# Attention in steps of two heads: row-tiled score matmuls and three rotating bank pairs, in a rewritten program

## The reference

```python
qkv = (x @ Wqkv.T + bqkv)                       # q, k, v: 16 heads of 16
attn = softmax(q @ k.T / 4)                     # 512 x 512 for each head and batch
coh = sigmoid(tanh([x, cond] @ Wc1.T + bc1) @ Wc2.T + bc2)
mod = attn * coh / ((attn * coh).sum(-1) + 1e-8)
fa = softmax(layernorm(relu(cond @ We1.T + be1) @ We2.T + be2) @ pe.T)   # a row per batch
out = (0.79 * mod + 0.21 * fa) @ v @ Wout.T + bout
x = x + out
x = x + rotate(x)      # a fixed 4 x 4 map of quarter features; the FFT pair with a real gate is a scale
```

## Time and profile before

| | us |
|---|---|
| median of 3 runs | 379.95 |
| lowest, highest | 377.29, 383.14 |
| the profiled execution, span from first to last instruction | 375.9 |
| mean granted TensorE clock in it | 0.904 of full |
| TensorE busy | 321.0 |
| VectorE busy | 223.9 |
| ScalarE busy | 176.9 |
| GpSimd busy | 156.8 |

### The profile page before, as it was taken

How to read it: one execution, slowest core, us unless ns; L and a number is a source line. 1 busy time by engine, 2 the same in 40 slices (tenths; PEclk the granted TensorE clock), 3 DMA queues, 4 the chain that set the end, 5 groups by cost and what they waited for, 6 DMA issues and landing times.

```text
span 375.9 us, 5338 instructions
## 1 busy us (share of the span) xinstructions
PE 321.0 (85%) x1537; PEld 189.0 (50%) x1537; DVE 223.9 (60%) x385; ACT 176.9 (47%) x323; POOL 156.8 (42%) x129
## 2 busy tenths in 40 slices
PE   0848849999799889999799689999799779999975
PEld 0634426555456456655456356655456346544423
DVE  3765943786568616687577407686577517775102
ACT  2101103765356625556456415565356525667750
POOL 9979950099991000299400000199500030296000
PEclk9986975999989958999899958999899969999996
DMA  8698498214953992216924991125943990200001
GB/s 245 247 125 99 146 127 123 83 58 99 125 59 112 126 163 51 75 66 127 124 30 145 149 118 36 62 78 112 118 51 122 124 146 1 84 1 2 1 1 57
DMA packets 16518, 35.87 MB, mean 95 GB/s; under 512 B 2724, under 2 KB 8228, under 8 KB 14456
## 3 DMA queue, kind: packets, MB, share of 16 engines
q1 hardware_dynamic: 14968, 34.47, 50.4%
q10 hardware_dynamic: 1536, 1.23, 1.2%
HBM read 25.07 MB, written 10.50 MB: 95 GB/s over the span
## 4 chain that ended last, share of the span: by engine, by line
PE 63%; DMA 24%; DVE 4%; ACT 3%; issue 3%; SPq 1%; ACTq 0%; DVEq 0%
PE smax_ps L996 14%; PE st_ps L1018 14%; PE o_ps L1030 13%; DMA stack<-max_rows 10%; DMA stack<-qk_scratch 10%; PE job_ps L894 9%; PE job_ps L929 3%; PE job_ps L970 3%; ACT probs L594 2%; DMA qk_scratch<-qk_lo 2%; PE job_ps L951 2%; DVE qk_lo L672 2%; PE smax_ps L982 2%; DMA w_raw<-wqkvT 1%; DVE maxima L746 1%
## 5 line engine op out<-in xcount | busy, mean ns | idle before, releaser
L746 DVE TENSOR_REDUCE maxima<-smax_ps 128x1 f32<-128x512 f32 x256 | 168.3, 686 | 113.6 <-PE smax_ps L996 113.0
L594 ACT ACTIVATE probs<-st_ps 128x512 f32<-128x512 f32 x247 | 142.6, 597 | 137.0 <-PE st_ps L1018 135.6
L996 PE MATMUL smax_ps<-stack 127*128 127x512 f32 x256 | 118.0, 464 | 13.8 <-DMA stack<-qk_scratch 11.9
L1018 PE MATMUL st_ps<-stack 128*128 128x512 f32 x247 | 107.7, 439 | 19.8 <-DMA stack<-max_rows 18.2
L996 PEld LDWEIGHTS smax_ps<-stack 127*128 127x128 f32 x256 | 52.0, 204 | 51.5 <-DVE maxima L746 24.4
L1030 PE MATMUL o_ps<-probs,vals 128*32 128x512 f32 x512 | 71.7, 634 | 1.0 <-ACT probs L594 0.9
L1018 PEld LDWEIGHTS st_ps<-stack 128*128 128x128 f32 x247 | 50.5, 205 | 39.6 <-DMA stack<-max_rows 19.8
L419 POOL TENSOR_TENSOR vals<-v_new,vals 128x256 f32<-128x256 f32 x16 | 10.0, 641 | 94.5 <-PE o_ps L1030 94.5
L401 POOL TENSOR_TENSOR x_lo<-x_raw,x_hi 128x1024 fp32r<-128x1024 f32 x3 | 7.2, 2388 | 65.7 <-ACT x_hi L550 65.7
L894 PE MATMUL job_ps<-x_hi,w_hi 128*128 128x512 f32 x48 | 22.0, 459 | 10.0 <-DVE w_lo L797 9.5
L519 POOL TENSOR_TENSOR prod<-amap,x_tok 128x1024 f32<-128x1024 f32 x12 | 28.6, 2383 | 0.9
(11 more groups left out here) (105 smaller groups left out, 305.5 us busy)
## 6 DMA issues: line engine op xcount, KB each, us to landing
stack<-qk_scratch SPq DMA_DIRECT2D x64, 256.0 KB, 9.7
qk_scratch<-qk_hi SPq DMA_DIRECT2D x16, 256.0 KB, 2.0
qk_scratch<-qk_lo SPq DMA_DIRECT2D x16, 256.0 KB, 2.0
x_tok<-x SPq DMA_DIRECT2D x4, 512.0 KB, 12.0
out<-y SPq DMA_DIRECT2D x8, 256.0 KB, 2.2
x_raw<-xT SPq DMA_DIRECT2D x3, 512.0 KB, 12.1
pe_tab<-fa_rows SPq DMA_DIRECT2D x4, 256.0 KB, 3.8
row<-rows SPq DMA_DIRECT2D x1, 936.0 KB, 7.6
```

The costliest lines, as they stand in the source:

```text
L594: nc.scalar.activation(probs[:, t % RING, :], st_bank(b, t)[:, :], ACT.Exp, scale=SCALE).then_inc(exp_done, 1)
L746: nc.vector.tensor_reduce(maxima[:, g % 2, n:n + 1], smax_ps[smax_bank(u)][:, :], AX_X, ALU.max).then_inc(smax_reduced, 1)
L996: nc.tensor.matmul(smax_ps[smax_bank(u)][:, :], stack[0:MAX_ROW, 0, h, i * P:(i + 1) * P], stack[0:MAX_ROW, 1, h, :], start=True, stop=Tru ...
L1018: nc.tensor.matmul(st_bank(b, t)[:, :], stack[:, 1, h, j * P:(j + 1) * P], stack[:, 0, h, :], start=True, stop=True).then_inc(st_filled, 1)
```

## The change

Nearly every function is rewritten; the computation stays.

- A step is now a pair of heads and one block of 128 rows: 32 steps a batch, 128 in all, unrolled for the four batches. There are 12 steps (`LEAD`) between S and T of the same index.
- `stack` holds two heads in one block: 48 rows (three combinations, lo-lo left out) from partition 0 and 48 from partition 64; T takes a 49th row, the maximum. A pair is two matmuls, one at each partition offset, into the two banks of a pair. Three pairs (`pair_ps`) rotate over the sequence T, S, T, S, ...; in a step T comes first. `slot_free` makes each wait for the reader of the pair used three events earlier.
- One reduce and one exponential cover both banks (1024 elements). The reduce negates.
- One bank `job_ps` for all jobs. Jobs are whole (no thirds) and placed by `JOB_STEPS` and `FIRST_STEPS`, behind the score matmuls and `weigh_values` of their step. `claim` waits for the readout of the job just before. For the jobs in `LATE` VectorE's readout comes one step later, behind that step's reduce.
- `stack` has three slots of half a batch (8 heads); a half is read with six DMAs of 256 KB and one semaphore.
- The first two pairs of heads of batch 0 are projected directly into `stack` (`direct`, plain fp32 from `w_dir`, low parts by two VectorE operations on 16 rows), so S can start without the trip through DRAM.
- The weights are split by GpSimd, not VectorE; the copies of `values` and others go to ScalarE. The logits `z` are computed transposed in four column tiles and transposed back (`zt`). The last batch's output is done whole at the end.

The core of the diff:

```diff
+PER_BATCH = G * IT * 2
+STEPS = B * PER_BATCH
+LEAD = 12
+TERMS = 3
+ROWS = TERMS * HD
+HALF_SLOTS = 3
+JOB_STEPS = {"q0": -20, "k0": -18, "q1": -6, "k1": -4, "v0": -2, "v1": 4, "coh0": 6, "coh1": 10, "z": 11, "zt": 13,
+             "max0": 9, "max1": 17, "max2": 25, "max3": 33, "field": 27,
+             "tok0": 24, "tok1": 32, "tok2": 40, "tok3": 48, "back0": 34, "back1": 50, "out0": 52, "out1": 54}
+FIRST_STEPS = {"q0": 0, "k0": 1, "dq1": 2, "dk1": 3, "q1": 4, "k1": 5, "cond": 6, "norms": 7, "fpre": 8, "v0": 9,
+               "v1": 11, "fpair": 14, "flog": 15, "coh0": 16, "coh1": 18, "z": 19, "zt": 21}
+BEFORE = ["dq0", "dk0"]
+LATE = ("q0", "q1", "k0", "k1", "out0", "out1")
+def weigh_at(n):
+    k, odd = divmod(n - LEAD - 3, 2)
+    return k if not odd and 0 <= k < STEPS // 2 else None
+def events():
+    order = []
+    for n in range(STEPS + LEAD):
+        if n >= LEAD:
+            order.append(("T", n - LEAD))
+        if n < STEPS:
+            order.append(("S", n))
+    return order
+EVENTS = events()
+SLOT = {event: n % 3 for n, event in enumerate(EVENTS)}
+AHEAD = {event: EVENTS[n - 3] for n, event in enumerate(EVENTS) if n >= 3}
...
+            def claim(job):
+                if PLACE[job]:
+                    wait(pe, *read_out(ORDER[PLACE[job] - 1]))
...
+            def slot_free(event):
+                if event in AHEAD:
+                    kind, n = AHEAD[event]
+                    pe.wait_ge(s_reduced if kind == "S" else exp_done, n + 1)
+
+            def scores_for_max(u):
+                gg, pair, i = u // 8, u % 8 // IT, u % IT
+                slot, turn = slot_of(gg // 2)
+                p = 4 * slot + 2 * (gg % 2) + pair
+                if gg == 0:
+                    if i == 0:
+                        pe.wait_ge(dir_lo_done, 4 * (pair + 1))
+                elif u % 16 == 0 or u == 8:
+                    pe.wait_ge(stack_loaded[slot], 96 * (turn + 1))
+                slot_free(("S", u))
+                for a in range(2):
+                    ins = nc.tensor.matmul(pair_ps[SLOT["S", u]][:, a, :],
+                                           stack[64 * a:64 * a + ROWS, 0, p, i * P:(i + 1) * P],
+                                           stack[64 * a:64 * a + ROWS, 1, p, :], start=True, stop=True)
+                ins.then_inc(s_filled, 1)
+
+            def scores(t):
+                gg, j, pair = t // 8, t % 8 // 2, t % 2
+                slot, _ = slot_of(gg // 2)
+                p = 4 * slot + 2 * (gg % 2) + pair
+                if t % 8 == 0:
+                    pe.wait_ge(max_loaded, 16 * (gg + 1))
+                slot_free(("T", t))
+                for a in range(2):
+                    ins = nc.tensor.matmul(pair_ps[SLOT["T", t]][:, a, :],
+                                           stack[64 * a:64 * a + ROWS + 1, 1, p, j * P:(j + 1) * P],
+                                           stack[64 * a:64 * a + ROWS + 1, 0, p, :], start=True, stop=True)
+                ins.then_inc(t_filled, 1)
...
+            for n in range(LAST_STEP + 1):
+                if LEAD <= n < STEPS + LEAD:
+                    scores(n - LEAD)
+                if n < STEPS:
+                    scores_for_max(n)
+                k = weigh_at(n)
+                if k is not None:
+                    weigh_values(k)
+                for job in JOBS.get(n, []):
+                    run_job(job)
```

The new readers and the order of SyncE's work:

```diff
+                nc.vector.tensor_reduce(maxima[:, gg % 2, :, pair, i], pair_ps[SLOT["S", u]][:, :, :], AX_X,
+                                        ALU.max, negate=True).then_inc(s_reduced, 1)
...
+                nc.scalar.activation(probs[:, t % 4, :, :], ps[:, :, :], ACT.Exp, scale=SCALE).then_inc(exp_done, 1)
...
+            for b in range(B):
+                if b + 1 < B:
+                    write_qk(2 * b + 2)
+                    read_stack(2 * b + 2)
+                if b == 0:
+                    sp.wait_ge(fatt_done, 1)
+                    sp.dma_start(fa_rows, fexp[:, :]).then_inc(fa_written, 16)
+                if b:
+                    store(b - 1)
+                load_field(b)
+                if b + 2 < B:
                     load_x(b + 2)
+                if b + 1 < B:
+                    write_qk(2 * b + 3)
+                    read_stack(2 * b + 3)
+                    load_tokens(b + 1)
```

More of the change, by code:

```diff
@@ L53 @@
[L53 to L80, removed]
@@ new lines, with jobs_by_step @@
+BEFORE = ["dq0", "dk0"]
+LATE = ("q0", "q1", "k0", "k1", "out0", "out1")
+def jobs_by_step():
+    table = {}
+    for b in range(B):
+        steps = {**JOB_STEPS, **(FIRST_STEPS if b == 0 else {})}
+        for name, step in steps.items():
+            table.setdefault(PER_BATCH * b + step, []).append((name, b))
+    return table
+JOBS = jobs_by_step()
+LAST_STEP = max(JOBS)
+ORDER = [(name, 0) for name in BEFORE] + [job for n in range(LAST_STEP + 1) for job in JOBS.get(n, [])]
+PLACE = {job: n for n, job in enumerate(ORDER)}
@@ L125, with slot_of, build @@
          [(-1, 2), (1, 3), (1, 0), (-1, 1)], [(-1, 3), (-1, 2), (1, 1), (1, 0)]]
[L128 to L142, removed]
 def wait(eng, sem, value):
-    if not (isinstance(value, int) and value <= 0):
+    if value > 0:
         eng.wait_ge(sem, value)
-def build(nc, x, xT, wqkvT, wc1T, wc2T, we2T, woutT, w64, rows, cols, pe_table, identity, fill, out):
+def slot_of(half):
+    return half % HALF_SLOTS, half // HALF_SLOTS
+def build(nc, x, xT, wdirT, wqkvT, wc1T, wc2T, we2T, woutT, w64, rows, small, cols, pe_table, identity, out):
     with ExitStack() as ctx:
@@ L243, in build @@
[L243 to L249, removed]
+        fa_now = sb("fa_now", [P, S])
@@ L286, in build, with wait_job, last_out @@
+                "fpair": (fpairT_done, 1), "flog": (fexp_done, 1),
+            }[name.rstrip("0123")]
+        def wait_job(eng, job):
+            wait(eng, job_filled, PLACE[job] + 1)
+        def last_out(job):
+            return job[0].startswith("out") and job[1] == B - 1
         block = ctx.enter_context(nc.Block())
@@ new lines, in project, with logits @@
+                ins.then_inc(job_filled, 1)
+            def logits(job):
+                claim(job)
+                b = job[1]
+                pe.wait_ge(h_ready, KT * (b + 1))
+                pe.wait_ge(ld_wc2, 16)
+                for k in range(KT):
+                    for i in range(IT):
+                        ins = nc.tensor.matmul(job_ps[i * VW:(i + 1) * VW, 0:P], wc2[:, k, :],
+                                               hT[:, k, i * P:(i + 1) * P], start=(k == 0), stop=(k == KT - 1))
+                ins.then_inc(job_filled, 1)
```

1208 lines of the change are left out of this document (535 added, 673 removed).

## The result

The changed kernel takes 394.97 us (median of 6 runs, 390.86 to 402.79) where the kernel before, beside it, takes 379.91 (6 runs, 377.29 to 386.35). The ratio is 1.035, with a 95% interval of 1.027 to 1.044: slower. The forecast was 383, and its range of 325 to 425 holds the result; the single value is 12 us low.

A forecast was written before the change was run, and what follows sets the result against it. TensorE, the DMAs that stop it and its clock were taken as the bound; opening 63, steps 224, waits 63, T alone 12.5 and end 16 sum to 379 us, plus 4 for the median: 383, range 325 to 425.

The forecast's parts named there:

- steps 12 to 128: Main stretch of 3.62 batches: 224 us undisturbed plus 63 us for six waits for the maxima.
- T alone: Twelve last steps with T but no S, paced by ScalarE: 12.5 us.
- tail: From the last weighing to the end, last output with 16 passes behind the last transposes: 16 us.
- Pairs of score matmuls: Two row-tiled matmuls run together at one matmul's cost: 15 us a batch where 30 stood.
- rival 2: Row tiles run one after the other, each pair 0.47 us, slower: 423 us; chance 0.12.
- A batch: 32 steps take 64 us undisturbed, 2.0 a step, against 71 before.
- Maxima and their DMA: max1 and max3 of batches 0 to 2 meet stack reads, land in 9 us; six waits of 6 us each.
- Rival 1: Faster: the maxima land in time, under 4 us, leaving six 1 us waits and no slow clock: 326 us; chance 0.26.
- Clock: After each of six waits TensorE runs 9 us at half clock, 4.5 us more per wait.
- rival 3: Slower: TensorE stays at 1.2 GHz from one wait to the next, 8 to 9 us more per wait, 434 us; chance 0.07.
- Opening: Before the first T: eight jobs through one bank at 4.5 us each, 36 in all; first T at 63 us, against 55.4.
- Late readouts: Claims waiting for readouts put a step later, behind that step's reduce, cost TensorE 3.5 us a batch.

The follow-up runs named there:

- the experiment with the tiles in turn: Changed kernel with both matmuls of every score pair reading the stack from partition 0, so they cannot run side by side: 464.5 us.
- the kernel with both edits: Changed kernel with k0 and k1 moved so stack reads follow the maxima's small DMA, and LATE emptied so no readout is a step late: 318.6 us.
- the throwaway matmuls: Changed kernel with 20 throwaway score pairs run on TensorE ahead of each of the six waits for max_rows: 381.7 us.
- With two banks: Changed kernel with the opening's jobs taking o_ps and job_ps in turn, each waiting for the job two before: 377.0 us.
- the empty list: Changed kernel with LATE emptied, so VectorE's readouts of q, k and out are not put off by a step: 379.1 us.
- the moved reads: Changed kernel with only job step numbers moved (k0, k1 later), so each half's stack reads start behind a maximum's small DMA: 345.9 us.
- the runs that were to tell: Changed kernel with only one half's reads put behind the maxima: first half (k0 moved) 376.2 us, second half (k1 moved) 391.1 us.
- when S goes first: S issued ahead of T in each step: 389.9 us on the changed kernel; 320.0 us on the kernel with two opening banks, later reads and empty LATE.
- the three edits together: Changed kernel with two banks in turn for the opening's jobs, stack reads behind the maxima and no readout a step late: 304.8 us.

## Why the prediction was right where it was, and where it missed

Its sum against the profiled span, term by term:

| term | forecast | measured | from |
|---|---|---|---|
| first T | 63 | 71.4 | T's first start |
| steps 12 to 128 | 287 | 293.5 | 71.4 to the last weighing of a step with S, 364.9 |
| T alone | 12.5 | 15.2 | to the last weighing, 380.1 |
| tail | 16 | 13.7 | to 393.8 |
| sum | 378.5 | 393.8 | |

**Pairs of score matmuls: right.** 0.24 taken, 0.24 measured, and the experiment with the tiles in turn costs the 0.23 a pair that rival 2 named.

**A batch: right in its sum, in part by luck.** With its two waits it was to take 64 + 2 x 10.5 = 85. From `z` of batch 1 at 158.94 to that of batch 2 at 244.47 it takes 85.5, then 85.2. In these two batches the four waits last 7.3 to 7.9 us, so two cost 15 and not 12. The clock is at 1.2 GHz for some 4.9 us behind each of them and for 3.4 more a batch elsewhere, which is 6.6 lost in all and not 9. That leaves 64 undisturbed, as forecast. The waits were too cheap by 3 and the clock too dear by 2.5, and the two cancel. Without waits and late readouts 60.5 were forecast; the kernel with both edits takes 62.6 and 61.5. Projection step, `tok` step (3.05 from weighing to weighing, forecast 3.3), reduce, exponential and the stop of 1.0 for `qk_lo` all stand.

**Maxima and their DMA: right in place and number, small in size.** Six waits, `max1` and `max3` of batches 0 to 2. A landing was taken at 9 and took 9.95 in the mean; a wait at 6 and took 6.7 (43.4 less the opening's 3.4, over six). Rival 1 is out: no landing was under 4. The rows for it were a median over DMAs issued with idle queues; the row that met fresh reads the earlier trace rows was the right one. The Trainium skill (DMA: Bandwidth & Descriptors, Queues, rings and completion order) states that a DMA engine takes turns between its queues packet by packet, by which 8 KB on ScalarE's queue would slip between SP's reads. No run here shows this: 7.3 to 11.0 behind reads, at most 3.1 to 4.4 ahead of them.

**Clock: right in kind, too dear in size.** It falls to 1.2 GHz at each wait. The windows tell when it is back, for the third and the sixth of the six as follows:

```profile
184.00:192.00 8.00, 7.66 (x34) 0.75 0.14 28
...
312.00:320.00 8.00, 7.49 (x35) 0.65 0.01 2
```

0.75 is 4 us at half, to 188.0, where T began at 183.3; 0.65 is 5.6 us, to 317.6, where T began at 312.5. Behind five of the waits work ran at half rate for 4.7 to 5.3 us, the rest of the slow stretch passed while TensorE stood; behind the first and shortest (3.3 us) it was 10. So rival 3 is out. Taken at 4.5 a wait, the slow clock costs 2.9 in the mean by these stretches and at least 2.2 by the throwaway matmuls. Short stops brought slow stretches of their own, which I had not priced.

**Opening: the step that failed.** The forecast let eight jobs pass through the one bank at 4.5 us each, with 1.5 for filling. They took from 5.65 to 52.4, 5.8 each: filling ran at 1.2 GHz and took 2.3 to 3.8. The rows of before showed fills at full clock, in a stream of other work; with one bank TensorE stands still between jobs. That is 10.7 us. The other terms nearly cancel: 1.0 less for x, 2.5 less for `q1`'s x, which nothing waited for, 3.5 more for the short jobs up to the small DMA, 2.0 less for its landing. The first T is 8.4 late, more than half of the 15.3 that the span is above the forecast. With two banks the first T comes 18.6 earlier, so the single bank cost more than the term was short by.

**Late readouts: right in a batch, short elsewhere.** 3.5 a batch, 12.7 in all, was the price in the batches. With the empty list a batch takes 82.1 (`z` at 148.68, 230.75 and 312.92) where it took 85.4, so 3.3. The empty list gave 16 alone and 27 beside the moved reads; 6 to 7 of either lie in the opening, and 5.9 of the 27 are stops that the move itself had brought.

**Tail:** 16 passes at 385.2 took 5.4, and their readout began while the last of them ran; 2.3 less than taken. From the span to the median I added 4, as in the kernel before; it was 1.2.

What stays open: how the 49 us of the moved reads split between the two halves, as the runs that were to tell have doubled steps, five in each; how much of the 11 us that the two edits give together is the clock; why the score pairs stand longer when S goes first; and by which order the DMA engines serve the two queues.

## What to carry to other kernels

A program that runs its scores at half the cost gained nothing, since a small transfer on which the next step depends was issued just behind bulk reads that nobody needed for 16 steps: order the issues by due time, over all queues. Then look for short stops too: one evacuation a step late, or one bank for all jobs, costs its microsecond and can cost the clock. Moving a job to cure one wait can bring another, as here behind `k0` and `k1`, so look at the waits again after each edit: the three edits together took 395 us to 305. And an order within a step that seems free while the kernel waits for DMAs is not free once it no longer does.

## What the hardware showed that was not expected

Stops of 0.99 and 1.56 us, with others shorter, in 8 us in which TensorE was busy 5.45, were followed by some 6 us at 1.2 GHz; no long wait is needed for it. An 8 KB DMA needs 7.3 to 11.0 us when six reads of 256 KB were issued 1 to 7 us ahead of it on another queue, and at most 3.1 to 4.4 when it is issued ahead of them, by 0 to 1.4 us. Two matmuls on row tiles at partitions 0 and 64, of 48 rows and 512 columns each, take 0.24 us together, and 0.23 more when both lie on the rows from partition 0.
